# A first batch's feed-forward work moved into the second pair's up stage, with weight conversion spread over three stages

## The reference

```
x = x + attention(layernorm(x), ctx) @ Wfc.T + bfc     # 32 query heads, 8 key groups, head size 16
x = x + (gelu(y @ w_gate0) * (y @ w_gate1)) @ w_linear  # y = layernorm(x); hidden 2048; fp8 inputs
```

## Time and the profile before

| | |
|---|---|
| median of 3 runs | 464.41 us (464.25 to 465.84) |
| the profiled execution | 465.95 us, of which the span of the trace is 463.75 us |
| PE busy | 430.3 us, 93% of the span |
| DVE, ACT, POOL busy | 334.6, 313.0, 236.4 us |
| mean granted clock of PE | 0.978 |

### The profile page before, as it was taken

The page is one execution under the profiler, slowest core; times in us unless marked ns, Lnnn a source line. Parts: engine busy times, 40 slices in busy tenths (PEclk is TensorE's granted clock), DMA queues, the critical chain, the costliest instruction groups (busy, mean ns, idle before and its releaser), DMA issues.

```text
span 463.8 us, 11802 instructions
## 1 busy us (share of the span) xinstructions
PE 430.3 (93%) x4620; PEld 346.0 (75%) x4620; DVE 334.6 (72%) x704; ACT 313.0 (67%) x578; POOL 236.4 (51%) x226
## 2 busy tenths in 40 slices
PE   7867969889999999999999999999999999899997
PEld 6746848767787877877787878877787878558973
DVE  4776587976897579966897579966897579575542
ACT  6848784987379745977379745977379744885541
POOL 5577982695228713684228813684228812492000
PEclk9967799999999999999999999999999999999999
DMA  7797769264602560045401551035401251000001
GB/s 286 283 255 287 230 182 294 79 206 133 161 3 56 152 136 28 3 98 152 116 4 37 152 142 39 3 94 156 118 3 42 76 126 37 3 24 24 3 25 45
DMA packets 21239, 49.79 MB, mean 107 GB/s; under 512 B 4672, under 2 KB 5184, under 8 KB 21184
## 3 DMA queue, kind: packets, MB, share of 16 engines
q1 hardware_dynamic: 20862, 48.24, 36.2%
q10 hardware_dynamic: 322, 0.80, 0.7%
HBM read 23.86 MB, written 4.19 MB: 60 GB/s over the span
## 4 chain that ended last, share of the span: by engine, by line
PE 62%; DVE 11%; issue 8%; POOL 8%; ACT 7%; DMA 2%; ACTq 1%; POOLq 0%; SPq 0%; DVEq 0%
PE bank L644 16%; PE bank L664 10%; PE bank L443 6%; PE bank L445 6%; PE bank L444 6%; PE bank L551 5%; POOL plo L1297 5%; PE bank L518 4%; DVE mneg L1081 4%; PE bank L478 3%; PE bank L569 2%; PE bank L571 2%; ACT phi L840 1%; DMA qs<-cq 1%; DVE prod L1146 1%
## 5 line engine op out<-in xcount | busy, mean ns | idle before, releaser
L1297 POOL TENSOR_TENSOR plo<-p,phi 128x512 f16<-128x512 f32 x128 | 149.8, 1181 | 60.9 <-ACT phi L840 59.9
L644 PE MATMUL bank<-x2T,wgate 128*128 128x128 fp8e4 x2048 | 131.3, 221 | 3.6 <-DVE xr L1159 3.2
L644 PEld LDWEIGHTS bank<-x2T,wgate 128*128 128x128 fp8e4 x2048 | 117.0, 99 | 19.2 <-issue 12.1
L837 ACT ACTIVATE p<-bank 128x512 f32<-128x512 f32 x128 | 77.6, 606 | 20.0 <-PE bank L551 19.6
L1081 DVE TENSOR_REDUCE mneg<-bank 128x4 fp32r<-128x512 f32 x128 | 84.4, 684 | 7.6 <-PE bank L518 7.2
L840 ACT ACTIVATE phi<-bank 128x512 f16<-128x512 f32 x128 | 77.4, 605 | 0.0
L664 PE MATMUL bank<-wlin,act 128*128 128x512 fp8e4 x256 | 72.4, 378 | 0.0
L859 ACT ACTIVATE gate<-bank 128x512 bf16<-128x512 f32 x64 | 38.2, 597 | 50.1 <-PE bank L644 37.3
L863 ACT CAST ff<-bank 128x512 bf16<-128x512 f32 x64 | 37.5, 587 | 49.3 <-PE bank L644 49.3
L518 PE MATMUL bank<-kmask,cq 128*128 128x512 f32 x128 | 58.1, 480 | 4.5 <-DVE mneg L1081 2.8
L551 PE MATMUL bank<-qs,ks 98*128 98x512 f32 x128 | 55.5, 434 | 5.1 <-ACT phi L840 2.5
(11 more groups left out here) (117 smaller groups left out, 813.2 us busy)
## 6 DMA issues: line engine op xcount, KB each, us to landing
qs<-cq SPq DMA_DIRECT2D x90, 128.0 KB, 2.5
stage<-in_w SPq DMA_DIRECT2D x14, 512.0 KB, 5.4
ks<-khl SPq DMA_DIRECT2D x96, 64.0 KB, 2.0
cin<-in_ctx SPq DMA_DIRECT2D x8, 512.0 KB, 4.4
xr<-in_x SPq DMA_DIRECT2D x16, 256.0 KB, 4.5
out<-xr SPq DMA_DIRECT2D x16, 256.0 KB, 2.7
xr<-in_w SPq DMA_DIRECT2D x6, 512.0 KB, 6.2
raw_g<-in_w SPq DMA_DIRECT2D x4, 512.0 KB, 5.9
```

The source lines that it names most:

```text
L644: mm = pe.matmul(out[:, h * SEQ:(h + 1) * SEQ], wgate8[:, UH * v + h, kk, part, :], x2T[:, b % NB, kk, :], start=kk == 0, stop=kk == KT - 1)
L837: act.activation(p32[:, e % P32BUF, :], T[n % 2][:, :], ACT.Exp, scale=QUARTER).then_inc(p32_ok, 1)
L1297: pool.tensor_tensor(plo[:, e % PBUF, :], p32[:, e % P32BUF, :], phi[:, e % PBUF, :], ALU.subtract).then_inc(plo_ok, 1)
```

## The change

- **Units.** Stage 0 has no up stage. The second pair's up stage has twelve units, for batches 0, 1 and 2, in the order (0,0) (1,0) (0,1) (1,1) (2,0) (2,1) (0,2) (1,2) (2,2) (0,3) (1,3) (2,3), written as (batch, quarter). `x2T` and `act8` have three buffers for that.
- **Down.** Batch 0's `down` moves from tile stage 1 to tile stage 2, which now has three; they lie in slots 0 to 5, 7 to 11 and 13 to 17.
- **Scores of the second pair.** The eight of its first batch lie in slots 12 to 18 of stage 0, the eight of its second batch in slots 0 to 3 of stage 1, two to a slot. Stage 1's preparations start four slots later than before (K at slots 4 and 5, Q at 11 to 18).
- **Weights.** 17 chunks go by POOL and ACT: two in tile stage 0, three in tile stage 1 and one per unit of the twelve-unit stage (POOL clamps these around its other work there). Seven go by DVE: three in stage 0, two at units 9 and 10, two in slots 1 and 2 of stage 2. The stage buffers are six instead of three.
- **SPq.** The loads are spread over stages 0 and 1, and x of pairs 2 and 3 is loaded earlier.
- **Small.** The selector rows of the second `ks` buffer are copied by a DMA instead of by ACT (L875). `dynamic_dma_scratch_size=1024` is given.

Where nothing else is said, pairs 2 to 7 keep their order.

```diff
-STAGES = 3
+STAGES = 6
-W_DVE = [8, 10, 12, 14, 16, 18, 20] + list(range(W_LIN, CHUNKS, 2))
-CLAMP_SLOTS = ((2, 5, 8, 10, 12, 14, 16), (3, 5, 8, 11))
-DVE_SLOTS = ((3, 5, 7, 9, 11, 13, 15), (3, 5, 8, 11))
+W_DVE = [5, 7, 9, 25, 26, 27, 28]
+W_CLAMPED = [6, 8, 12, 10, 11] + list(range(13, 25))
+CLAMP_SLOTS = ((3, 9), (1, 4, 8))
+DVE_SLOTS = {0: (3, 8, 10), 2: (1, 2)}
+DVE_UNITS = (9, 10)
+ABUF = 3
+PLAN_0 = dict(max=3, k=(0, 1), v=(2, 3), x=(5, 6), q=tuple(range(7, 15)), norm=0, even=None,
+              early={12: 1, 13: 1, 14: 1, 15: 1, 16: 2, 17: 1, 18: 1}, m_early={13: 1, 14: 1, 15: 1, 16: 1, 17: 1, 18: 2, 19: 1},
+              chain=dict(turn=13, project=(14, 15, 16, 17), residual=18, rstd=18, norm=18, turn2=19))
+PLAN_1 = dict(max=5, k=(4, 5), v=(6, 7), x=(8, 9), q=tuple(range(11, 19)), norm=4, even=17,
+              early={16: 1, 17: 1, 18: 1}, m_early={17: 1, 18: 1},
+              chain=dict(turn=0, project=(8, 9, 10, 11), residual=12, rstd=12, norm=13, turn2=15))
+S_SECOND = 4
+M_UNIT = 5
...
+def units(p):
+    if p == 1:
+        order = ((0, 0), (1, 0), (0, 1), (1, 1), (2, 0), (2, 1), (0, 2), (1, 2), (2, 2), (0, 3), (1, 3), (2, 3))
+        return list(order)
+    return [(b, v) for b in up_batches(p) for v in range(UPB)]
+def unit_scores(p, k):
+    if p == NP - 1 or p == 0:
+        return ()
+    if p == 1:
+        return (3, 4) if k == 0 else (k + 4,)
+    return tuple(s for s in (2 * k, 2 * k + 1) if s >= 4)
...
@@ sync
+            def copy_select():
+                sp.wait_ge(sel_in, 1)
+                sp.wait_ge(q_done, 2)
+                sp.dma_start(ks[SROWS:P, 1, :, :, :].bitcast(F32), ks[SROWS:P, 0, :, :, :].bitcast(F32)).then_inc(sel_copied, 16)
...
                     for hp in range(PAIRS):
                         stack_k(q, hp)
+                    if p == 0:
+                        load_chunk(11)
+                        load_chunk(12)
                     if q + 1 < NP:
                         load_ctx(q + 1)
+                if p == 0:
+                    load_chunk(13)
+                    load_chunk(14)
+                    load_x(2)
+                    load_chunk(15)
+                    load_chunk(16)
...
@@ tensor
                 for n in range(SLOTS):
                     if n < TILES:
                         scores_t(p, n)
+                    if p == 1 and n < S_SECOND:
+                        for s in (2 * n, 2 * n + 1):
+                            scores(p, 1, s)
...
+                if p == 0:
+                    turn_max(1, 0)
@@ scalar
                     gate_out(u)
...
                     ff_out(u)
+                    if p == 1:
+                        chunk_cast(clamped.pop(0))
```

More of the change, by code:

```diff
@@ L95, in units_through @@
 def units_through(p):
-    return UPB * sum(len(up_batches(r)) for r in range(p + 1))
+    return sum(len(units(r)) for r in range(p + 1))
 def chain_in_e(b):
@@ L425, in _ @@
                         stack_q(q, hp)
[L426 removed]
+                for b in late[len(first):]:
                     store(b)
[L428 to L429 removed]
+                if p == 1:
+                    for c in range(19, 27):
                         load_chunk(c)
```

344 lines of the change are left out of this document (172 added, 172 removed).

## The result

The changed kernel takes 472.07 us (median of 4 runs, 471.02 to 473.37), the kernel before beside it 465.12 (464.25 to 466.25, 4 runs): a ratio of 1.0141, 95% interval 1.0107 to 1.0175. It is slower by 1.4%; the forecast of 462.6 and its range up to 469 are both missed.

What follows compares the result with a forecast made beforehand. PE was taken to bound from stage 2 on, POOL tile stage 1, with waits and lower clock in stage 0. 71.5 + 28.0 + 30.1 + 56.6 = 186.2 against 188.00 gave 462.6 us, range 457 to 469.

Steps and rivals of the forecast that it cites:

- T1: Start of pair 1's first `scores_t`: predicted at 71.5 us, before 82.64; bounds 67.5 and 76.
- T3: Start of pair 3's first `scores_t`: predicted at 186.2 us, before 188.00.
- About 17 us are lost in it, to waits and to the lower clock: Stage 0, tile and up stage: 53.2 us taken against 35.7 us of PE work.
- The queue reckoning: DMA queue ahead of T1: 4.2 MB of loads to 63.4, then queries to 70.0 us.
- Tile stage 1: Pair 1's tile stage: 28.0 us, before 30.72; bounds 26.6 and 30.7.
- Up stage 1: Pair 1's twelve units: 30.1 us, before 22.33 with eight; bounds 29.5 and 33.
- rival 3: Twelve units run at the converting engines' pace, 2.4 instead of 2.10 us: 465, or 466 with late chunks; chance 0.12.
- My sum for DVE: Twelve-unit stage: DVE takes 1.50 + 0.47 = 1.97 us a unit beside clamps, hidden under PE's 2.10.
- Stage 2: Pair 2's tile and up stage: 56.6 us, before 52.3; 3.5 for the down, 0.8 for late casts.
- Rival 1: Early hand-over: PE keeps 2.4 GHz in stage 0, T1 67.5 to 69, time 458.5 to 460; chance 0.20.
- Rival 2: Weight loads hold up queries and maxima at the hand-over; T1 at 76 gives 467; chance 0.16.
- Rival 4: Nothing gained: stages 1 and 2 give back exactly what T1 won, 464.4; chance 0.10.

Runs made afterwards that it cites:

- e16: e13 with maxima ahead of batch 0's residual, 24 instead of 46 transposes at the hand-over and 20 in slot 7 of tile stage 0; 467.10 us.
- e12: Changed kernel with e3, e4, e9 and earlier maxima of pair 1 together, all work done; 467.30 us, ratio 1.0033.
- e3: Changed kernel with pair 1's second maxima in bank G0, so that V no longer takes the keys' bank; 470.51 us, ratio 1.0108.
- e6: Changed kernel with 14 of the 16 matmuls of batch 0's down left out; 472.29 us, ratio 1.012.
- e4: Changed kernel with 46 extra transposes into a free bank, keeping the array busy at the hand-over; 470.40 us, ratio 1.0109.
- e7: Changed kernel with no weight converted (zeros written, ACT casts 8 columns), loads kept; 468.08 us, ratio 1.0047.
- e1: Changed kernel with POOL's clamps of chunks 13 to 24 cut to 8 of 1024 columns; 475.82 us, ratio 1.0206.
- e2: Changed kernel with nearly all conversion from chunk 13 on removed, loads kept; 469.19 us, ratio 1.0078.
- e13: e12 with two more clamps and two casts moved into earlier idle gaps of POOL and ACT in the twelve-unit stage; 465.16 us, ratio 0.9997.
- e11: Changed kernel without the clamp and cast of chunks 23 and 24 on POOL and ACT; 469.63 us, ratio 1.0086.
- e10: Changed kernel with DVE writing zeros instead of converting chunks 27 and 28; 472.66 us, ratio 1.0146.
- e14: e13 with DVE converting chunks 13 and 14 in tile stage 1 and none in tile stage 2; 465.07 us, ratio 0.9993.
- e9: Changed kernel with batch 2's x turned behind unit 3's second half and its x2T written ahead of gelu 3; 471.15 us, ratio 1.0125.
- e17: Kernel before, with 20 added transposes in slot 7 of tile stage 0; 466.02 us, ratio 1.0004.

## Why the prediction was wrong

**The step that failed** is the pricing of the three stages behind T1. The sum had 28.0 + 30.1 + 56.6 = 114.7 us from T1 to T3, each stage as its full engine's work and hardly a wait; measured are 30.55 + 32.18 + 58.63 = 121.4. That is 6.7 of the 7.1 us by which T3 missed. The median missed by 9.5 us, the traced execution by 6.9 (471.02 against 464.15), since it is the fastest of four.

**What bounds the kernel** was read rightly in part: all edits act ahead of pair 3, and the periods behind it stayed (52.28 us). Of the sentence "About 17 us are lost in it, to waits and to the lower clock" the change got back little. By the prediction's own prices 9.6 us of PE work left stage 0 (7.3 for the units, 8 x 0.28 for the second batch's scores), and T1 came 10.7 us earlier. Work that moves in this way is paid again where PE is full, and there it was paid with waits on top.

**T1** was right, 71.94 for 71.5, and so was what releases it (the maxima's DMA). Its closeness is in part luck, for T1 lay between 70.67 and 74.21 in eight executions with this stage 0. The queue reckoning behind it was sound too, with one row misread: the rates of 348 to 376 GB/s in the earlier trace rows stand at 68.4 to 70.8 us, behind the first queries' issues, and at 66 to 68 us there are 109 to 225. In e16, where the loads were issued later, its other outcome appeared.

**Tile stage 1** was mis-sized: 30.55 for 28.0. The prediction added up POOL's work and took PE's as the lower bound, 26.6; with two costs gone e12 came to 28.30. The first is a wait that the change adds: V's projection behind the keys' low part in one bank, with DVE late by the second batch's maxima. The prediction read the slots of the edit but not its order of banks, and the sentence that POOL's subtraction "nearly hides" those maxima is wrong in its consequence. e3 shows 0.94 us for it. The second is the clock: the sum has no price for 1.2 GHz behind the waits of the hand-over, which was granted until 77.1. It cost 1.3 us (e6 against e4, e3 against e12).

**Up stage 1** was mis-sized: 32.18 for 30.1. The wait that was put at nothing is that for batch 2's second norm, ahead of unit 4: 1.45 us for the normalised x and 0.93 for its turned copy, 2.4 in all, more than the whole miss. From there on the forecast pace held. PE took a unit in 2.08 to 2.09 us, once in 2.33, so rival 3's mechanism cost 0.24 us, and e7, with nothing converted, is 0.25 us shorter over these units. ACT's gelus came later by the unit, 2.29 us apart from 119.07 to 135.09, but PE did not wait for them. My sum for DVE, 1.97 of 2.10 us, took the added clamps' price from the product; in the trace the conversion of the product bears most of it, 888 ns on the average against 529 in e1, and the place where POOL's work beside DVE reached PE is batch 2's normalisation (1.26 us against 0.55). All conversions away: 1.0 us (e2). All conversions kept and better placed, with batch 2's chain out of the way: 1.5 us (e13). The place counted for more than the number.

**Stage 2** was mis-sized: 58.63 for 56.6, all of it in the tile stage, 6.39 us longer. Its parts: 4.15 are left with nothing converted (34.12 - 29.97 in e7), which holds the third down and the new order of the slots and which no run splits (I took 3.5 for the down, with 3.8 as its most; e6, without most of the down, is only 0.22 shorter), 1.41 for late casts and 0.85 for the DVE chunks (e11, e10). I had 0.8 for the first cast effect, within the bound of 1.7, and "hide" for the DVE chunks, from an average busy time: 21.36 of 29.97 over the stage says nothing of slots 1 and 2.

**The rivals.** Rival 1's condition did not come: PE ran at 1.2 GHz at 43.0 to 49.8, as at 44.4 to 51.2 in the kernel before. Where that stretch was 3.4 us shorter, T1 was 1.3 to 1.7 us earlier (e11 against the changed kernel, e14 against e13), and in e11 tile stage 1 kept its length, so its mechanism is real. Rival 2 was not the cause, though its mechanism exists (e16). Rival 3 was not the cause either: late chunks held PE in e9 and e12, for 1.0 and 1.1 us, and the pace of the converting engines 0.24. Rival 4 had the nearest idea, that the later stages give back what T1 wins, and was too mild: they took 16.0 (121.36 from T1 to T3 against 105.34) where T1 won 10.7. That all three later terms were priced well under their upper bounds is the common error; the upper bounds, 30.7, 33 and 52.3 + 3.8 + 1.7 = 57.8, with T1 as predicted, add up to 193.0, and the measured start was 193.3.

**What the change is worth when mended.** e13 does all the work and is level with the kernel before (0.9997). Its account from the earlier trace rows: T1 12.0 us earlier, tile stage 1 2.4 shorter, the units 8.4 and tile stage 2 5.3 longer, 0.8 us in all. No version that does all the work beats the kernel before by a measurable amount. Of these mends only the transposes in slot 7 were tried in the kernel before (e17).

Open: why e1's clock fell in the units (PE had waited 1.84 us for batch 2's x there); what decides, between executions of one stage 0, where the low clock lies; what the third down costs alone; and whether an order with clear queues and e13's tile stage 1 (68.7 + 28.3 + 30.7 + 34.8) would hold together, which only adding lengths of different runs suggests.

## What to carry to other kernels

Price a move against the work that it takes along. Here T1 came 10.7 us earlier and 9.6 us of PE work had left, so nearly all of the gain was a debt to the next stages, and these have a full PE: they took 16.0 us more. A stage that looks slack on the average can hold its loss elsewhere; take away what is suspected (here the conversions, in both orders) and see in which slots the time goes.

Removing one suspect says little where two lie close together, and the stage's length alone can mislead: a down of 2.8 us of PE time left out changed 0.2, and a low clock cured at the hand-over won 1.2 us by slot 7 and lost it to another stretch behind that. Compare slot by slot before calling a cause worthless, and read each run's clock.

When work is put at the end of a stage, ask what the engine's next stage needs first (a table load, a first exponential), and look in the same trace for idle stretches of that engine further ahead: e13 moved the same casts into them for 2 us.
